# Attention scores taken out of the widened layer products, shifts in three rounds, in a three-layer graph attention kernel

## The chip, the cores and the metric

The kernel runs on one core of a Trainium2 chip. The metric is the time of the device in microseconds (us), the median of several runs; lower is better. The engines are TensorE (PE), VectorE (DVE), ScalarE (ACT), GpSimd (POOL) and SyncE (SP, which here only issues transfers). Each works through its own instructions in order, and they wait for one another by semaphores.

## The reference

1250 nodes with 768 features, 41250 edges and a self loop for each node. One dense layer gives x1; three graph attention layers (GAT) of four heads with 192 channels each all read x1, so there are 12 heads; their outputs are joined, multiplied by W_out, and added to x before a layer norm.

```python
def gat_conv(x, src, dst, W, a_src, a_dst, b):
    h = (x @ W).reshape(N, H, C)
    as_n = (h * a_src).sum(-1)
    ad_n = (h * a_dst).sum(-1)
    e = leaky_relu(as_n[src] + ad_n[dst], 0.2)
    m = segment_max(e, dst, num_segments=N)
    p = exp(e - m[dst])
    s = segment_sum(p, dst, num_segments=N)
    alpha = p / (s[dst] + 1e-16)
    out = segment_sum(alpha[:, :, None] * h[src], dst, num_segments=N)
    return out.reshape(N, H * C) + b
x1 = relu(x @ W_ah + b_ah)
xs = [relu(gat_conv(x1, src, dst, W, a_s, a_d, b)) for the three layers]
y = relu(concatenate(xs, axis=1) @ W_out + b_out)
return layernorm(x + y)
```

## The kernel before

The nodes are cut into 10 tiles of 125 (NT, PT), the 768 features into 6 blocks of 128 (KT, KP). The attention is dense: a matrix of edge counts (`cntT`, 1250 x 1250) and a mask (a very negative number where no edge is) are made once, then each head's weights are a full 1250 x 1250 matrix of exponentials times counts.

**Stage 1, to about 129 us.** PE counts edges into tiles and makes x1 (`x1_step`), in 18 groups: (m, 0) for all m, then (m, 1), (m, 2) in turn. ACT writes each group twice, as f32 (`x1T`) and rounded (`x1_hi`). DVE makes one-hot keys and then V = W a for each head (`reduce_v(l, k)`, eight reductions for each layer l and block k; SP loads the rows of W, three slots).

**Scores.** With V of all 12 heads (24 columns, source and destination), PE makes `scores(k)`: 36 f32 matmuls of x1T by V into `asadT`, 24 x 1250. ACT copies it out, SP stores the source rows to DRAM (`as_dram`), and PE turns it back to `asad` (nodes by heads) in `scores_turn`.

**Layer parts, 141.8 to 338 us.** `h_part(n)`, n = 0 to 5 (layer n // 2, half n % 2 of its columns): for each tile, 18 products of 384 columns into one PSUM bank (x_hi by W_hi, x_hi by W_lo, x_lo by W_hi, for 6 blocks). ACT copies each tile out, and after each odd tile issues two stores to `h_dram`. The weights of part n+1 are cast to `Wl_hi` by ACT (`round_w`, after tile ROUND_AT) from the raw ones, and DVE makes the rest (`rest_w`). The raw half of part n+2 is loaded after the last tile of part n. In part 0 stands an edge pass for windows with many edges (`more_counts`), a handshake of SP, DVE, PE and ACT.

**Maxima, on DVE beside the parts.** For each head a row of source scores is broadcast to all partitions (`asB`, SP's `load_as`), and 10 scans (L957) add the mask and take the maximum over the sources. Heads 0 to 9 (DEFER) come before the first shifts; heads 10 and 11 are scanned inside the first four pairs (`late_max`, five scans in each pair at LATE_AT).

**Shifts.** From the maxima DVE makes two numbers per node and head (`u`); PE turns them (`shifts`), ACT copies, SP stores to `u_dram` and broadcasts them back as rows (`load_u`). The first round, heads 0 to 9, is in part 5 after tile U_AT; the second, heads 10 and 11, before pair 4, where PE waits until ACT has copied the last features (`attT_sb`), because both use the same PSUM banks.

**Pairs of heads, 338 to 750 us.** For p = 0 to 5, 20 tiles each: DVE makes the exponent (`exponent_tile`), ACT the exponential, DVE the weight (`weight_tile`), PE 20 products of 193 columns (`tile`). There are two exponent slots and five weight slots. After each head DVE takes the sums (`invert`), ACT scales the head's output out of PSUM (`head_out`), and PE turns the features (`features`). Pairs 0 to 3 run in a loop on PE and ACT.

**End, 750 to 955 us.** W_out and the layer norm.

The order on each engine is written out by hand. The lines that the steps touch:

```python
def h_products(n, t, blocks):
    place = bank((2 * (n % 2) + t) % 4)[0:PT, 0:HALF]
    for k in blocks:
        if n == 0 and t == 0:
            pe.wait_ge(S["x1_lo"], k + 1)
            pe.wait_ge(S["w_lo"], 1)
        for i, (xx, ww) in enumerate(((x1_hi, Wl_hi), (x1_hi, Wl_lo), (x1_lo, Wl_hi))):
            ins = mm(place, xx[:, k, t * PT:(t + 1) * PT], ww[n][:, k], ...)
```

Of the kernel before, what the change touches and what calls it, by code (L numbers as in the profile page):

```python
# [14 lines left out]
PT = 125  # L15
# [27 lines left out]
V_HEAD = 1  # L43
G0_PARTS = 3
# [9 lines left out]
DEFER = LH - 2  # L54
TAKEN = 2 * NT // (PAIRS - 2)
# [3 lines left out]
ROUND_AT = 4  # L59
# [4 lines left out]
U_AT = 2  # L64
EXP_AT = NT - 3
# [36 lines left out]
def gnn_program(nc, x, xT_rows, dst, edges, W_ah, b_ah, W_all, a_all, b_all, W_out, b_out, out):  # L102
# [10 lines left out]
    with ExitStack() as ctx:  # L113
# [98 lines left out]
        asadT, _ = view(R_ROWS, 2 * N, 2 * LH, (N,))  # L212

        w_at = [(0, 7504)] + [(4808, 2504), (0, 7504)] * 2 + [(4808, 2504)]
        Wl_hi = [rounded("Wl_hi0", "R_EXP", 0, (KT, HALF))]
        Wl_hi += [rounded(f"Wl_hi{n}", "R_W", w_at[n][0], (KT, HALF)) for n in range(1, PARTS)]
        Wl_lo = [rounded(f"Wl_lo{n}", "R_W", w_at[n][1], (KT, HALF)) for n in range(PARTS)]
        w_raw = [view(R_W, w_at[n][1], KP, (KT, HALF))[0] for n in range(PARTS)]
# [63 lines left out]
        def out_at(q, t):  # L282
# [64 lines left out]
        def _(sp):  # L347
# [48 lines left out]

            def load_as(hh):
# [31 lines left out]
            for q in range(2):  # L429
                load_h(0, q)  # L430
            sp.wait_ge(S["h_ps"], NT * PARTS)
# [11 lines left out]
            with sp.Fori(1, PAIRS - 2) as p:  # L443
                load_pair(p)
            load_pair(PAIRS - 2)

            sp.wait_ge(S["uT_sb"], 2 * len(GROUPS))
            for w in range(2):
                rows = slice(w * LH + DEFER, (w + 1) * LH)
                sp.dma_start(u_dram[rows], uT2[rows]).then_inc(S["u_stored"], 16)  # L450
            sp.wait_ge(S["u_stored"], 16 * 3)
# [44 lines left out]
        def _(pool):  # L496
# [52 lines left out]
            pool.wait_ge(S["u_stored"], 16 * 3)  # L549
# [5 lines left out]
        def _(act):  # L555
# [84 lines left out]
            act.wait_ge(S["v_made"], 2 * HEADS * KT * LAYERS)  # L640
            act.wait_ge(S["asad_ps"], KT)
            for g, (t0, w) in enumerate(GROUPS):
                nc.scalar.copy(asadT[:, t0 * PT:(t0 + w) * PT], bank(2 + g)[0:2 * LH, 0:w * PT]).then_inc(S["asadT_sb"], 1)
            round_w(1)
# [25 lines left out]

            def h_part(n):

                l, c = n // 2, n % 2
                for t in range(NT):
                    i, slot = 5 * c + t // 2, (5 * c + t // 2) % 2
                    act.wait_ge(S["h_ps"], NT * n + t + 1)
                    if t % 2 == 0:

                        act.wait_ge(h_stored[slot], 32 * (NT // 2 * l + i // 2 + 1))
# [766 lines left out]
```

## Time and profile before

| | |
|---|---|
| Time before, median of 3 runs | 956.46 us (956.26 to 956.62) |
| Profiled execution | 956.7 us; span from its first to its last instruction 955.1 us |
| Granted TensorE clock, mean | 0.999 |
| PE busy | 933.2 us (98%) |
| DVE busy | 739.1 us (77%) |
| ACT busy | 367.5 us (38%) |
| DMA | 108.16 MB, mean 113 GB/s |

The profile is of one execution, the times are of others. Busy times are unions of overlapping instructions, and a matmul's record is longer than the step from one to the next, so counts and steps say more than means. "Idle before" is what the engine waited for, named by the one who released it. All times are us from the span's start unless marked ns.

### The profile page before, as it was taken

Reading aid. Unit: us, or ns where it says so; the run is one execution under the profiler, and the core shown is the slowest. Engines: PE = TensorE matmul, PEld = TensorE weight load, DVE = VectorE, ACT = ScalarE, POOL = GpSimd, SP = SyncE. Lnnn points to the kernel's source line nnn. Section 1 sums busy time; section 2 is a strip of 40 time slices with the busy share of each in tenths; the row PEclk is TensorE's granted clock in tenths of the full one; section 3 lists DMA queues with packets and bytes.
Section 4 is the critical chain, followed back from the end, with each engine's and each line's share of the span. In section 5 each row is a group of like instructions: output and inputs, shape, how many; then the busy total and the mean of one; then the engine's idle time right before and its main releaser. Section 6 shows DMA issues by size and latency. Waiting matters only on the chain.

```text
span 955.1 us, 14393 instructions
## 1 busy us (share of the span) xinstructions
PE 933.2 (98%) x5584; PEld 865.8 (91%) x5584; DVE 739.1 (77%) x1064; ACT 367.5 (38%) x534; POOL 45.9 (5%) x94
## 2 busy tenths in 40 slices
PE   6999999999999999999999999999999999999997
PEld 2677649999999999999999999999999779999996
DVE  6999986999999299998999999988877282243233
ACT  1666323122212255375465555555555540011000
POOL 4700000000000000000010010010010100000000
PEclk9999999999999999999999999999999999999999
DMA  5350722534453723144253352239341353223111
GB/s 174 50 197 22 259 85 89 168 108 152 130 163 92 227 75 95 56 108 106 82 123 63 94 131 67 71 101 374 93 121 42 101 161 127 81 91 116 68 33 33
DMA packets 57693, 108.16 MB, mean 113 GB/s; under 512 B 14013, under 2 KB 41246, under 8 KB 56487
## 3 DMA queue, kind: packets, MB, share of 16 engines
q1 hardware_dynamic: 39188, 66.22, 22.7%
q0 software_dynamic: 5360, 18.77, 7.7%
q10 hardware_dynamic: 13090, 22.44, 7.5%
q8 instruction: 34, 0.56, 0.2%
q14 instruction: 21, 0.16, 0.1%
HBM read 80.34 MB, written 27.08 MB: 112 GB/s over the span
## 4 chain that ended last, share of the span: by engine, by line
PE 56%; ACT 0%; DVE 0%; issue 0%; ACTq 0%
PE ps L1302 34%; PE ps L1382 18%; PE ps L1372 2%; PE ps L1337 2%; ACT R_XIN L733 0%; PE ps L1287 0%; DVE R_XIN L1118 0%; DVE stats L1108 0%; DVE R_EXP L1104 0%; DVE R_EXP L1102 0%; ACT rstd L785 0%; DVE mv L1113 0%; DVE rstd L1115 0%; ACTq L732 0%; ACTq L762 0%
## 5 line engine op out<-in xcount | busy, mean ns | idle before, releaser
L1302 PE MATMUL ps<-R_W 125*125 125x193 f32 x2400 | 395.2, 327 | 1.2 <-issue 0.8
L1302 PEld LDWEIGHTS ps<-R_W 125*125 125x125 f32 x2400 | 391.7, 188 | 1.8 <-issue 1.1
L707 ACT ACTIVATE R_W<-R_EXP,s 125x1250 f32<-125x1250 f32 x120 | 160.3, 1340 | 155.0 <-PE ps L1302 74.7
L998 DVE SCALAR_TENSOR_TENSOR R_W<-R_W,R_CNT 125x1250 f32<-125x1250 f32 x120 | 174.5, 1455 | 3.0 <-DVE R_EXP L987 1.7
L957 DVE CUSTOM_DVE_ANT_0 R_ROWS<-R_MASK,R_ROWS 125x1250 bf16<-125x1250 bf16 x100 | 138.6, 1456 | 3.2 <-ACTq L660 3.2
L1230 PE MATMUL ps<-Wl_hi,x_hi 128*125 128x384 f32 x360 | 122.1, 339 | 0.0
L1230 PE MATMUL ps<-Wl_hi,x_lo 128*125 128x384 f32 x360 | 121.7, 338 | 0.0
L1230 PE MATMUL ps<-Wl_lo,x_hi 128*125 128x384 f32 x360 | 121.6, 338 | 0.0
L1382 PE MATMUL ps<-Wo_hi,xs_hi 128*125 128x384 f32 (+2 forms) x324 | 109.5, 338 | 0.3 <-PE ps L1372 0.3
L1382 PE MATMUL ps<-Wo_lo,xs_hi 128*125 128x384 f32 (+2 forms) x324 | 109.4, 338 | 0.0
L1382 PE MATMUL ps<-Wo_hi,xs_lo 128*125 128x384 f32 (+2 forms) x324 | 109.2, 337 | 0.0
L987 DVE SCALAR_TENSOR_TENSOR R_EXP<-R_EXP,s 125x1250 f32<-125x1250 f32 x60 | 90.8, 1515 | 20.8 <-DMA R_EXP<-u_dram 12.3
L987 DVE SCALAR_TENSOR_TENSOR R_EXP<-R_X,s 125x1250 f32<-125x1250 f32 x60 | 90.7, 1511 | 13.4 <-ACT R_W L707 12.8
L1102 DVE TENSOR_TENSOR R_EXP<-ps,R_EXP 125x768 f32<-125x768 f32 (+2 forms) x11 | 9.7, 885 | 99.1 <-PE ps L1382 99.1
L680 ACT COPY R_HOUT<-ps 125x384 f32<-125x384 f32 x60 | 28.9, 481 | 140.3 <-PE ps L1230 138.7
L1174 PE MATMUL ps<-R_W 128*128 128x500 f32 (+1 forms) x180 | 74.8, 546 | 7.6 <-DMA R_W<-in_xT 7.6
L1230 PEld LDWEIGHTS ps<-Wl_hi,x_hi 128*125 128x125 f32 x360 | 66.8, 185 | 0.5 <-issue 0.4
L1230 PEld LDWEIGHTS ps<-Wl_lo,x_hi 128*125 128x125 f32 x360 | 66.7, 185 | 0.0
L1230 PEld LDWEIGHTS ps<-Wl_hi,x_lo 128*125 128x125 f32 x360 | 66.7, 185 | 0.0
L785 ACT ACTIVATE rstd<-mv,epsc 125x1 f32<-125x1 f32 x10 | 3.0, 296 | 158.6 <-DVE mv L1113 158.6
L1382 PEld LDWEIGHTS ps<-Wo_hi,xs_hi 128*125 128x125 f32 x324 | 60.0, 185 | 1.8 <-issue 0.9
L1382 PEld LDWEIGHTS ps<-Wo_lo,xs_hi 128*125 128x125 f32 x324 | 60.1, 185 | 0.9
(146 smaller groups left out, 824.8 us busy)
## 6 DMA issues: line engine op xcount, KB each, us to landing
xs_dram<-R_XIN POOLq DMA_DIRECT2D x18, 625.0 KB, 8.6
h_dram<-R_HOUT ACTq DMA_DIRECT2D x30, 336.0 KB
R_W<-h_dram SPq DMA_DIRECT2D x12, 840.0 KB
R_ROWS<-as_dram SPq DMA_DIRECT2D x12, 625.0 KB, 4.4
R_EXP<-u_dram SPq DMA_DIRECT2D x6, 1250.0 KB, 7.8
R_X<-u_dram SPq DMA_DIRECT2D x6, 1250.0 KB, 5.6
R_ROWS<-in_W_all SPq DMA_DIRECT2D x18, 384.0 KB, 3.4
Wo_sb<-in_W_out POOLq DMA_DIRECT2D x1, 6912.0 KB, 27.0
```

The costliest lines, as they stand in the source:

```text
L680: nc.scalar.copy(h_out[:, slot, t % 2 * HALF:(t % 2 + 1) * HALF], bank((2 * c + t) % 4)[0:PT, 0:HALF]).then_inc(S["h_sb"], 1)
L707: nc.scalar.activation(prob[r % PSLOTS], expo[:, r % XSLOTS], ACT.Exp, bias=s02[:, r % NT, ds(2 * p + r // NT, 1)]).then_inc(S["exp_done"], 1)
L957: nc.vector.tensor_tensor_reduce(out=masked[:, i % 2], in0=mask[:, b], in1=asB[0:PT, hh % 2], scale=1.0, scalar=NOBODY, op0=ALU.add, op1=A ...
L987: nc.vector.scalar_tensor_tensor(out=expo[:, r % XSLOTS], in0=uB[q][0:PT, 0], scalar=s08[:, r % NT, ds(2 * p + q, 1)], in1=uB[q][0:PT, 1], ...
L998: nc.vector.scalar_tensor_tensor(out=prob[r % PSLOTS], in0=prob[r % PSLOTS], scalar=HUGE, in1=cntT[:, r % NT, 0:N], op0=ALU.min, op1=ALU.m ...
L1102: nc.vector.tensor_tensor(yt_part, y_part, bo_part, ALU.add).then_inc(S["y_sum"], 1)
L1174: ins = mm(bank(5 + i % 3)[:, 0:w], W_ah_sb[m][:, k], xT[g][:, k], start=(k == 0), stop=(k == KT - 1))
L1230: ins = mm(place, xx[:, k, t * PT:(t + 1) * PT], ww[n][:, k], start=(k == 0 and i == 0), stop=(k == blocks[-1] and i == 2), skip_group_che ...
L1302: ins = mm(ps[0:PT, o:o + HW], prob[(q * NT + j) % PSLOTS][:, t * PT:(t + 1) * PT], hB[:, q, j], start=(j == 0 and t % 2 == 0), stop=(j == ...
L1337: ins = nc.tensor.transpose(bank(5 + i)[:, t * PT:(t + 1) * PT], att[:, g + t, k * KP:(k + 1) * KP], ident[0:PT, 0:PT])
L1372: ins = mm(ps[0:PT, o:o + HALF], xs_first[:, k] if k < early else xsT[:, k - early, 0:PT], Wo_sb[:, k, c * HALF:(c + 1) * HALF], start=(k ...
L1382: ins = mm(place, xx[i][:, k], ww[:, k, half], start=(k == 0 and n == 0), stop=(k == OK - 1 and n == 2))
```

## The change

- **Scores as columns.** `scores` and `scores_turn` go. V of the first two layers (heads 0 to 7, 16 columns) is set beside the weights of part 0, and V of layer 2 (heads 8 to 11, 8 columns) beside those of part 1, rounded and with a rest as the weights are (`round_v`, `rest_v`). The products of part 0 have 400 columns, those of part 1 392. ACT copies the score columns of each tile to `asad`; PE turns the source columns back (`source_turn`: eight tiles after tile 8 of part 0, two in the middle of the first tile of part 1, and ten after the first tile of part 2 for layer 2).
- **Order in part 0.** PE makes the x_hi terms of tiles 0 and 3 before it needs x1_lo; x1_lo is made for a group of tiles at a time (`rest_x1`), and V of layer 2 after V of the others, two of its blocks ahead of the edge pass and four behind it.
- **Weights.** The raw half of part n+1 is now loaded after tile 1 of part n, cast after tile 5 (ROUND_AT 5), and its rest is made at written-out places among the scans (REST_W_AT).
- **Shifts in three rounds.** Heads 0 to 7 after their 80 scans (turned in part 5 after tile 4), heads 8 and 9 in pair 1 (their 20 scans follow the first shifts), heads 10 and 11 before pair 4. Each of the later rounds has its turn on PE, copies on ACT, and two stores on SP.
- **First exponents.** `exponent_tile(0, 0)` and `(0, 1)` stand before the scans 6 and 7 of head 9, the weight tiles 0 and 1 before its scans 8 and 9.
- Pairs 0 and 1 are written out on PE and ACT, the loop runs over pairs 2 and 3.

```diff
-ROUND_AT = 4
+SCORED = [2 * ROUND_A, 2 * HEADS]
+REST_W_AT = {(0, NT - 1): 2, (3, 0): 3, (5, 0): 4, (7, 1): 5}
+EXP_IN = 6
+ROUND_AT = 5
+RAW_AT = 1
-U_AT = 2
-EXP_AT = NT - 3
+U_AT = 4
+EXP_AT = NT - 2
...
             def round_w(n):
-                act.wait_ge(S["w_in"], 16 * n + 16)
-                nc.scalar.copy(Wl_hi[n][:], w_raw[n]).then_inc(S["w_hi"], 1)
+                act.wait_ge(S["w_in"] if n else S["w_in_first"], 16 * max(n, 1))
+                nc.scalar.copy(Wl_hi[n][:, :, 0:HALF], w_raw[n]).then_inc(S["w_hi"], 1)
+            def round_v(n):
+                act.wait_ge(S["v_made"], 2 * HEADS * KT * (2 + n))
+                nc.scalar.copy(score_columns(n, Wl_hi), V_part[n]).then_inc(S["v_hi"], 1)
...
-                    if t == NT - 1 and n + 2 < PARTS:
-                        act.dma_start(w_raw[n + 2], w_half(n + 2)).then_inc(S["w_in"], 16)
-                    if t == ROUND_AT and 1 <= n < PARTS - 1:
+                    if t == RAW_AT and 1 <= n < PARTS - 1:
+                        act.dma_start(w_raw[n + 1], w_half(n + 1)).then_inc(S["w_in"], 16)
+                    if t == ROUND_AT and n < PARTS - 1:
                         round_w(n + 1)
...
+            dve.wait_ge(S["mask_ready"], 2 * NT + 1)
+            for hh in range(DEFER):
+                dve.wait_ge(asB_in[hh % 2], 16 * (hh // 2 + 1))
+                for b in range(NT):
+                    i = NT * hh + b
+                    if (hh, b) in REST_W_AT:
+                        rest_w(REST_W_AT[hh, b])
+                    if (hh, b) == (4, 0):
+                        slopes()
+                    if hh == DEFER - 1 and EXP_IN <= b < EXP_IN + XSLOTS:
+                        exponent_tile(0, b - EXP_IN)
+                    if hh == DEFER - 1 and b >= EXP_IN + XSLOTS:
+                        weight_tile(0, b - EXP_IN - XSLOTS)
...
+                if hh == ROUND_A - 1:
...
+                    shifts(0, ROUND_A, z)
...
+                    if late == (0, 1) and r == ROUND_B_AT:
+                        dve.wait_ge(S["uT_ps"], len(GROUPS))
+                        shifts(ROUND_A, DEFER, z)
...
             def h_part(n):
                 pe.wait_ge(S["w_hi"], n + 1)
-                if n > 0:
+                if n == 0:
+                    pe.wait_ge(S["v_hi"], 1)
+                    hi_terms(0)
+                    hi_terms(3)
+                    lo_terms(0).then_inc(S["h_ps"], 1)
+                    more_counts()
+                else:
                     pe.wait_ge(S["w_lo"], n + 1)
...
-            with pe.Fori(0, PAIRS - 2) as p:
+            pair(0, False)
+            pe.wait_ge(S["attT_sb"], 9 + 1)
+            shifts(2)
+            pair(1, False, nth=1)
+            with pe.Fori(2, PAIRS - 2) as p:
                 pair(p, False)
```

## Rows read from the trace of the kernel before

**Rows 1.** Stretches: us, then busy time of each engine (instructions), PE clock, DMA.
```profile
163.00:314.00 151.00, 151.00 (x861) 150.91 (x860) 146.66 (x205) 31.01 (x52) 0.14 (x1) 1.00 0.43 132
338.70:427.80 89.10, 88.64 (x551) 88.27 (x552) 87.91 (x76) 47.21 (x57) 1.96 (x2) 1.00 0.30 82
929.75:942.33 12.58, 12.58 (x56) 10.01 (x55) 3.99 (x7) 0.29 (x1) 0.00 (x0) 1.00 0.10 32
```

**Rows 2.** Chain that ended last, in order of time: start, us, what.
```profile
426.76 1.07 PE ps L1337 x10
...
632.46 0.44 PE ps L1337 x4
...
635.82 58.83 PE ps L1302 x360
```

**Rows 3.** Timeline of PE: start, us, line, out<-in, count, [idle before, releaser].
```profile
129.08 12.77 PE L1211 MATMUL ps<-R_X,u_place 128*24 128x500 f32 x36 [1.10 <-issue]
...
145.13 1.26 PE L1238 MATMUL ps<-ident,R_ROWS 24*125 24x24 f32 x10
...
148.01 1.12 PE L1131 MATMUL ps<-R_W 128*125 128x120 f16 x16
...
151.18 0.79 PE L1158 MATMUL ps<-ident,R_ROWS 125*125 125x125 f16 x10 [0.95 <-DVE R_ROWS L922]
...
408.67 3.54 PE L1302 MATMUL ps<-R_W 125*125 125x193 f32 x20 [0.46 <-ACT R_XIN L722]
```

**Rows 4.** Timeline of DVE.
```profile
128.90 2.56 DVE L928 TENSOR_TENSOR Wl_lo<-R_W,Wl_hi 128x2304 fp32r<-128x2304 f32 x1
...
144.16 0.18 DVE L853 CAST R_EXP<-R_EXP 128x32 f32<-128x32 int32 x1 [0.74 <-issue]
...
291.94 2.56 DVE L928 TENSOR_TENSOR Wl_lo<-R_W,Wl_hi 128x2304 fp32r<-128x2304 f32 x1 [1.51 <-ACT Wl_hi L633]
...
312.67 0.26 DVE L971 TENSOR_TENSOR u_place<-R_ROWS 125x100 f32<-125x100 f32 x1
...
325.19 2.95 DVE L987 SCALAR_TENSOR_TENSOR R_EXP<-R_EXP,s 125x1250 f32<-125x1250 f32 x2 [12.26 <-DMA R_EXP<-u_dram]
...
342.20 1.45 DVE L998 SCALAR_TENSOR_TENSOR R_W<-R_W,R_CNT 125x1250 f32<-125x1250 f32 x1
...
407.38 0.22 DVE L1008 TENSOR_SCALAR rsum<-ps 125x4 f32<-125x4 f32 x2
```

**Rows 5.** Timeline of ACT; ACTq is its queue of transfers.
```profile
128.39 0.46 ACT L605 ACTIVATE x_hi<-ps,b_ah_sb 128x250 fp32r<-128x250 f32 x1
...
178.62 0.48 ACT L680 COPY R_HOUT<-ps 125x384 f32<-125x384 f32 x1 [2.68 <-PE ps L1230]
179.13 0.81 ACTq L685 DMA_DIRECT2D h_dram<-R_HOUT  x2
...
289.78 2.12 ACT L633 CAST Wl_hi<-R_W 128x2304 fp32r<-128x2304 f32 x1
```

**Rows 6.** Groups by line, DVE: count, busy us, mean ns, idle before.
```profile
L957 DVE CUSTOM_DVE_ANT_0 R_ROWS<-R_MASK,R_ROWS 125x1250 bf16<-125x1250 bf16 x100 | 138.6, 1456 | 3.2 <-ACTq L660 3.2
...
L839 DVE CUSTOM_DVE_ANT_0 R_EXP<-R_ROWS 128x192 bf16<-128x192 f32 x96 | 27.1, 355 | 2.5 <-DMA R_ROWS<-in_W_all 2.5
```

**Rows 7.** Timeline of SP's queue of transfers.
```profile
130.90 0.34 SPq L393 DMA_DIRECT2D R_EXP<-in_edges  x1
...
143.26 0.36 SPq L403 DMA_DIRECT2D as_dram<-R_ROWS  x1
...
145.29 42.49 SPq L400 DMA_DIRECT2D R_ROWS<-as_dram  x4
```

**Rows 8.** DMA issues: count, KB each, median us to landing.
```profile
R_ROWS<-as_dram SPq DMA_DIRECT2D x12, 625.0 KB, 4.4
...
R_EXP<-in_edges SPq DMA_DIRECT2D x1, 16.0 KB, 2.8
```

**Rows 9.** Timeline of PE at the start.
```profile
7.63 3.67 PE L1174 MATMUL ps<-R_W 128*128 128x500 f32 x4 [7.63 <-DMA R_W<-in_xT]
```

More of the change, by code:

```diff
@@ L395, in _ @@
                                  ).then_inc(S["more_in"], 16)
+            for k in range(V_AHEAD, KT):
+                load_v(2, k)
             def load_as(hh):
@@ L430, in _ @@
                 load_h(0, q)
+            for hh in range(DEFER, LH):
+                load_as(hh)
             sp.wait_ge(S["h_ps"], NT * PARTS)
@@ L639, in _ @@
                     round_w(0)
[L640 to L644, printed above, removed]
+                    round_v(0)
             act.sem_inc(S["exp_done"], XSLOTS)
@@ new lines, in _, with slopes @@
+            reduce_v(2, V_TURN - 1)
+            more_counts()
+            rest_x1(1, 0, KT)
+            rest_x1(2, 0, KT)
+            for k in range(V_TURN, KT):
+                reduce_v(2, k)
+            rest_w(1)
+            rest_v(1)
+            def slopes():
+                dve.wait_ge(S["asad_sb"], 2 * NT)
+                nc.vector.tensor_scalar(s08[:], asad[:, :, 0:LH], 1.0 - SLOPE, None, ALU.mult)
+                link(nc.vector.tensor_scalar(s02[:], asad[:, :, 0:LH], SLOPE, None, ALU.mult))
+                dve.sem_inc(S["scores_ready"], 1)
@@ L972, in shifts @@
                 dve.sem_inc(S["amax_done"], 1)
-            for w in range(2):
-                link(nc.vector.memset(u[:, :, w * LH + DEFER:(w + 1) * LH], 0.0))
-            shifts(0, DEFER, z)
             def exponent_tile(p, r):
@@ L1217, in _, with h_product @@
             pe.wait_ge(S["mask_ready"], 2 * NT)
-            pe.wait_ge(S["v_made"], 2 * HEADS * KT * LAYERS)
-            for k in range(KT):
-                scores(k)
+            TERMS = ((x1_hi, Wl_hi), (x1_hi, Wl_lo), (x1_lo, Wl_hi))
+            def h_product(n, t, k, i, last):
+                xx, ww = TERMS[i]
+                return mm(bank((2 * (n % 2) + t) % 4)[0:PT, 0:w_wide[n]], xx[:, k, t * PT:(t + 1) * PT], ww[n][:, k],
+                          start=(k == 0 and i == 0), stop=last, skip_group_check=True)
@@ L1222, in h_products @@
             def h_products(n, t, blocks):
-                place = bank((2 * (n % 2) + t) % 4)[0:PT, 0:HALF]
                 for k in blocks:
-                    if n == 0 and t == 0:
-                        pe.wait_ge(S["x1_lo"], k + 1)
-                        pe.wait_ge(S["w_lo"], 1)
-                    for i, (xx, ww) in enumerate(((x1_hi, Wl_hi), (x1_hi, Wl_lo), (x1_lo, Wl_hi))):
-                        ins = mm(place, xx[:, k, t * PT:(t + 1) * PT], ww[n][:, k],
-                                 start=(k == 0 and i == 0), stop=(k == blocks[-1] and i == 2), skip_group_check=True)
@@ new lines, in h_products, with hi_terms, lo_terms @@
+                return ins
+            def hi_terms(t):
+                for i in range(2):
+                    if i == 1:
+                        pe.wait_ge(S["w_lo"], 1)
+                        pe.wait_ge(S["v_lo"], 1)
+                    for k in range(KT):
+                        h_product(0, t, k, i, False)
+            def lo_terms(t):
+                pe.wait_ge(S["x1_lo"], 1 + (t >= 4) + (t >= 8))
+                for k in range(KT):
+                    ins = h_product(0, t, k, 2, k == KT - 1)
+                return ins
@@ L1242, in more_counts, with source_turn @@
+            def source_turn(n, heads, groups):
+                for g, w in groups:
+                    pe.wait_ge(S["asad_sb"], NT * n + g + w)
+                    for tt in range(w):
+                        ins = nc.tensor.transpose(bank(5 + GROUPS.index((g, w)))[0:heads.stop - heads.start, tt * PT:(tt + 1) * PT],
+                                                  asad[:, g + tt, heads], ident[0:PT, 0:PT])
+                    ins.then_inc(S["asT_ps"], 1)
             def more_counts():
```

204 lines of the change are left out of this document (124 added, 80 removed).

## The prediction, before the result was known

> **What bounds the kernel now.** I read the stretches first [rows 1]. From 163 to 314 us, the body of the six layer parts, TensorE (PE) is busy in every us: 861 products in 151.0 us, 175.4 ns from one start to the next. From 338.7 to 427.8 (pair 0 of heads) it is busy for 88.64 of 89.10, but VectorE (DVE) is busy for 87.91: in this one pair both are full. The chain of waits confirms PE from pair 1 on [rows 2]. So us taken from PE count only if DVE, which makes the weights for the pairs, is earlier too. The PE timeline shows the one place where PE waits for it in pair 0: 0.46 us at 408.67 [rows 3], right after DVE's sums at 407.38 [rows 4]. DVE runs without a gap from the third weight tile (342.20, next start 343.57) to 407.38 [rows 4]. That chain is the second limit, and it sits almost on top of the first.
>
> **Step 1, PE up to part 4.** The 36 score matmuls start at 129.08 and last 12.77 us [rows 3]; V of all layers ends when 128.90 begins [rows 4], so V is just in time for them. Without them part 0 needs the last x1 copy (128.39 + 0.46 = 128.85 [rows 5]) and starts at about 128.95. Before, its first product stood at 141.78, where the score row ends: -12.8 us. The first weight half was cast by then, and V of layers 0 and 1 is there: layer 2's 48 reductions take 48 x 0.28 = 13.5 us [rows 6], so the others ended by 115.5. Group 0 of x1_lo is 3000 elements, 3.3 us at the rate of the 2304 in 2.56 [rows 4]; it, two blocks of layer 2's V and the first rest of the weights fit before 128.5. The last four blocks (9 us) come after the edge pass, by 157, and V's second cast at tile 7 of part 0, by 163; part 1 wants both at 168.
>
> The ten turns of the scores go: -1.3 [rows 3].
>
> Wider products: 54 products of 512 columns start within 12.58 us, 233.0 ns each (the row counts two neighbours at its edges too); against 175.4 for 384 that is 0.45 ns per column [rows 1]. 16 columns x 180 = +1.3 us, 8 x 180 = +0.6. From below, nothing (if the weight load set the pace); the 512s exclude it.
>
> The later edge pass is a handshake, and it loses its cover. Its edges are sent for at 130.90 [rows 7] and land 2.8 us later [rows 8], 133.7; SP does the same work up to there. DVE needs 3.85 us from its first key operation (144.16) to PE's edge product (148.01) [rows 3, 4]: 137.6. PE comes there after 39 products of 182.5 ns, at 136.2. So it waits 1.4 us where it waited for nothing. From there to the mask block is 3.17 us as before (151.18), whose 0.95 us wait stays, near 1.1. +1.5 in all; from 0.5 to 2.5 if the edges land 1 us off.
>
> Source turns: ten turns last 1.26 us, the first of them overlapped [rows 3]; eight, two and ten make 0.9 + 0.3 + 1.1 = +2.3. Each waits for a copy of a tile that was done before, so they stop nothing behind them.
>
> Sum at the start of part 4: -12.8 - 1.3 + 1.3 + 0.6 + 1.5 + 2.3 = **-8.4**.
>
> **Step 2, DVE up to the first shifts.** Scores leave with part 0's tiles, so all ten must be done: PE ends part 0 near 167.8, turns the last group in the middle of the next tile (169.6), ACT copies, SP stores and waits (2.03 us from its last store, 143.26, to the load at 145.29 [rows 7]), and the row lands 4.4 us after issue [rows 8]: the first maximum at about 176.6. Eight heads are 80 x 1.386 = 110.9 [rows 6], four rests of weights about 10, slopes and shifts 2.4: 299.5 if nothing waits.
>
> But rests wait for ACT's casts, which move from the fifth tile to the sixth (ROUND_AT 5), an odd one, with two stores first. The last one before: part 4's fifth-tile copy is followed by the cast from 289.78 to 291.90 [rows 5], and DVE waited 1.51 for it [rows 4]. After: one tile later (+3.16), the copy to the end of the stores +1.32 (178.62 to 179.94) instead of +0.37 [rows 5], and -8.4: 287.6. DVE itself would be there (the second scan of head 7) at 282.5 had it never waited; so it waits at the casts, 1 to 2 us each time, and the last cast sets it. A later first maximum, by up to 4 us, costs nothing. Then 2.5 + 9 scans 12.5 + shifts 1.9: shifts are done at **304.5**. Before: 312.67 + 0.26 = 312.93 [rows 4]. -8.4, as PE.
>
> **Step 3, from the shifts to pair 0.** Before, DVE then waited 12.26 us for the rows of u [rows 4]. Twenty scans (heads 8 and 9) are put there: +27.7, less what it waited. The third weight tile comes after 20 scans, five exponents and three weights. A pair of the two is 2.82 us (63.8 us from 343.57 to 407.38 less five scans and 0.45, by 20), so these are 3 x 2.82 + 2 x 1.45 = 11.3: 304.5 + 27.7 + 11.3 = 343.5, against 343.57. The gain is gone: the order brought 8.4 us, and the waits that twenty scans fill were that long and no longer. The rows of u are in time. Before, PE turned them after part 5's third tile, eight tiles of 3.16 us behind the copy that precedes the cast at 289.78: 314.7, and the exponent began at 325.19, 10.5 us later. Now it is the fifth tile, two more, less 8.4: 312.6 + 10.5 = 323.1; the first exponent is due at 326.7. SP has nothing in front of them but head 9's row, sent for at 302. On ACT the first exponential (x at 328.2) stands in front of the last tile's copy, which PE has ready only at 329.5.
>
> PE, free at about 330, gets weight tile 0 at 333.9 (18 scans, two exponents, one weight after 304.5), so it idles near 3.5 us, 0.5 before tile 1 and 2.5 before tile 2. Pair 0 keeps its five late maxima, so DVE runs on to the sums at 407.3, and PE, which would be back at 406.5, passes at 408.6. **-0.1.**
>
> **Step 4, the third round of shifts.** PE must wait until the last features are copied, then turn ten tiles. Before, it does this once: the last features start at 632.46, pair 4 goes on at 635.82; without a round they last 1.07 (426.76) [rows 2]. 635.82 - 632.46 - 1.07 = **+2.3**. It is bare PE time in the pair boundary, and DVE does not bind there. DVE's own shifts (1.9) in pair 1 stand before tiles that PE wants only after its pause; ACT's and SP's parts lie in slack (SP's store of u stands before a load that waits for DVE anyway), and POOL, whose load of W_out now waits for five stores, is past them by then. If PE's features were copied earlier the price would be 1.2, if the pause met another wait it would be 3.5.
>
> **Sum.** -0.1 + 2.3 = +2.2 us. The profiled execution was 956.7 us (span 955.1), so 958.9; the median of the runs was 956.46: **958.5 us**. 0.2% is 1.9 us, about what can be told from no change.
>
> **A rule against the change.** The first four x1 matmuls, after 7.63 us of idle, took 3.67 us, 0.92 each [rows 9], and 500 columns settle at 0.42 later (12.77 us for 24 of 500 and 12 of 250 in [rows 3]): half the speed, the 1.2 GHz level instead of 2.4 (the granted clock of the whole run is 0.999, so it says little of so short a stretch). The new waits of 3.5 and 2.5 us could bring this back in pair 0. Lost then: 2.0 us, as there, to 3.5. PE has 2.1 us to spare up to 408.6, so 0 to 1.4 us would show.
> The Trainium skill, "TensorE: Matmul & The Clock Gate", section "Part 1: The HAM clock gate", says that an idle array goes back to the half clock and earns the full one by steady work; by it the time would be up to 959.9. Whether the trace agrees can't be read from it: after the start PE waits 1.1 us at most.
>
> **Rivals.**
> 1. *The casts don't hold DVE.* If they come before DVE does, the shifts are ready at 299.5 to 302.5 and everything in step 3 is 2 to 5 us earlier. PE then passes at 403.6 to 406.6: -2.1 + 2.3 = +0.2, down to -5.1 + 2.3 = -2.8. 953.6 to 956.7. For it: waits of 1 to 2 us are near my error. Against: before, two casts already held DVE by 1.4 and 1.5 us, at a tile earlier.
> 2. *PE keeps its gain* (the other side): DVE doesn't bind in pair 0, because its late maxima or weights find room. Then -8.4 + 2.3 = -6.1: 950.4. The 0.46 us at 408.67 speaks against it; it decides as soon as the sums come more than 1.9 us earlier than 407.3.
> 3. *A hand-over is late*: the first row of sources after 181, u after 326.7, or the clock above. Each us late passes through DVE to pair 0. +1.5 to +4 on the sum: 960 to 962.5.
> 4. *The edge pass waits longer than 1.4 us*: part of my range, +1.
>
> **How the numbers follow.** The chain as worked out, 956.8 to 959.8, has 0.48: the error is a us on the casts and half a us on the pause. Rival 3 with 4: 0.22. Rival 1: 0.18. Rival 2: 0.12. Range **953.6 to 962.5**: out are rival 2, a little of rival 1 and the end of rival 3, under 2 in 10. Below 954.5 lie rival 2 and a part of rival 1: faster 0.20. Above 958.4 lie half of the likeliest case and rival 3: slower 0.44. The rest, 0.36, is within 0.2%. Likeliest by itself: 956.8 to 959.8.
>
> **What would show it.** Part 0's first product near 129; a PE wait of 1.4 us before the edge product and 1 before the mask block; PE ahead by 8.4 us at part 4; the last cast ending near 287.6 and a DVE wait before each rest of weights; shifts done at 304.5; PE idle for some 3.5 us near 330; the sums of pair 0's second head at 407.3; pair 1's pause of 1.1 us and ten turns. I am wrong if shifts come before 302, if PE isn't idle before its first head tile, or if the pause is hidden.

## The result, and the profile after

The changed kernel takes 957.99 us (median of 22 runs, 957.61 to 959.05) against 956.20 (median of 22, 955.28 to 956.62): ratio 1.0021, 95% interval 1.0016 to 1.0027. So it is slower by 1.8 us, right at the 0.2% that the prediction took as the bound. Predicted were 958.5, in the likeliest case 956.8 to 959.8, in all 953.6 to 962.5. Of all the executions in this text one, of the kernel with narrow late maxima, took 2448 us; it is left out of its median.

The profiled execution has a span of 956.3 us (before 955.1). In it the last copy of x1 begins at 127.66, in before's at 128.39 [rows 5]. In the twelve other executions profiled below it begins anywhere from 127.28 to 129.05, so these 0.73 us are taken to belong to the execution and not to the change, and are put back where two times are compared ("so counted"). The change does move some loads and small operations ahead of that moment; no run tests them alone.

The timeline of TensorE (PE) in the changed kernel, where the edge pass, the start of pair 0 and the pass to pair 1 lie. "The pass" is the short wait at 407.62, where the banks of the last head must be free; the first 24 products of pair 1 stand just ahead of it. Products are counted by their records in the profile: the f32 matmuls of the pairs leave two each, so the 20 products of a weight tile are ten matmuls of the kernel (2400 records for 1200 of them).

```profile
128.34 1.32 PE L1302 MATMUL ps<-Wl_hi,x_hi 128*125 128x400 f32 x6 [1.08 <-issue]
136.83 1.17 PE L1217 MATMUL ps<-R_W 128*125 128x120 f16 x16 [1.09 <-DVE R_W L923]
140.06 0.79 PE L1244 MATMUL ps<-ident,R_EXP 125*125 125x125 f16 x10 [0.91 <-DVE R_EXP L980]
...
327.99 0.34 PE L1302 MATMUL ps<-Wl_hi,x_lo 128*125 128x384 f32 x1
332.85 8.29 PE L1418 MATMUL ps<-R_W 125*125 125x193 f32 x40 [4.52 <-DVE R_W L1058]
342.67 30.33 PE L1418 MATMUL ps<-R_W 125*125 125x193 f32 x184 [1.53 <-DVE R_W L1058]
373.48 32.95 PE L1418 MATMUL ps<-R_W 125*125 125x193 f32 x200 [0.48 <-ACT R_XIN L777]
407.62 9.42 PE L1418 MATMUL ps<-R_W 125*125 125x193 f32 x56 [1.19 <-ACT R_XIN L777]
...
427.83 1.24 PE L1403 MATMUL ps<-ident,u_place 125*24 125x125 f32 x10 [1.06 <-ACT R_XIN L788]
```

The layer parts are done at 328.33. Then stand a gap of 4.52 us, two weight tiles, a gap of 1.53 before the third, and two short ones (0.48 and 1.19) where ScalarE (ACT) copies a head out after VectorE's (DVE's) sums. The same stretch in the kernel before, read now from its timeline of PE:

```profile
337.58 0.34 PE L1230 MATMUL ps<-Wl_hi,x_lo 128*125 128x384 f32 x1
338.68 69.52 PE L1302 MATMUL ps<-R_W 125*125 125x193 f32 x424 [0.77 <-issue]
408.67 9.42 PE L1302 MATMUL ps<-R_W 125*125 125x193 f32 x56 [0.46 <-ACT R_XIN L722]
```

There all 424 products up to the pass run in one piece, 164.0 ns each. From the last product of the layer parts to the pass into pair 1 before needs 408.67 - 337.92 = 70.75 us, after 407.62 - 328.33 = 79.29. That is where the gain of the layer parts went: 8.54 us. Of it 3.75 are the first gap (4.52 - 0.77), 1.53 the second, 1.21 those at the sums (0.48 + 1.19 - 0.46), and 1.73 are the first 40 products, which took 8.29 in place of 6.56; 0.3 is left. A piece ends with a record that is longer than a step (28 products at the full clock took 4.84 us in the run with the gap filled, 0.25 more than 28 x 164.0 ns), so of the 1.73 nearer 1.5 are the clock's. The windows of the changed kernel show why the 40 were slow; the column after the busy times of the five engines is PE's granted clock:

```profile
332.00:333.00 1.00, 0.15 (x1) 0.18 (x2) 1.00 (x2) 0.00 (x0) 0.00 (x0) 0.76 0.96 299
333.00:334.00 1.00, 1.00 (x4) 1.00 (x5) 1.00 (x1) 0.00 (x0) 0.00 (x0) 0.50 0.93 357
334.00:335.00 1.00, 1.00 (x5) 1.00 (x4) 1.00 (x3) 0.00 (x0) 0.00 (x0) 0.50 0.38 138
335.00:336.00 1.00, 1.00 (x5) 1.00 (x4) 1.00 (x2) 0.00 (x0) 0.00 (x0) 0.54 0.00 0
336.00:337.00 1.00, 1.00 (x8) 1.00 (x7) 1.00 (x3) 0.00 (x0) 0.00 (x0) 1.00 0.00 0
```

By finer windows the granted clock is 0.50, the 1.2 GHz level, from about 332.5 to 335.9, that is from within the gap; the expectations below put it at 332.8 to 335.5.

The timeline of DVE in the changed kernel, against [rows 4]:

```profile
175.21 1.46 DVE L1089 CUSTOM_DVE_ANT_0 R_ROWS<-R_MASK,R_ROWS 125x1250 bf16<-125x1250 bf16 x1 [13.53 <-DMA R_ROWS<-as_dram]
190.33 2.56 DVE L993 TENSOR_TENSOR Wl_lo<-R_W,Wl_hi 128x2304 fp32r<-128x2304 f32 x1 [2.61 <-ACT Wl_hi L668]
223.29 2.56 DVE L993 TENSOR_TENSOR Wl_lo<-R_W,Wl_hi 128x2304 fp32r<-128x2304 f32 x1 [1.41 <-ACT Wl_hi L668]
254.88 2.56 DVE L993 TENSOR_TENSOR Wl_lo<-R_W,Wl_hi 128x2304 fp32r<-128x2304 f32 x1 [0.85 <-ACT Wl_hi L668]
...
303.06 0.24 DVE L1036 TENSOR_TENSOR u_place<-R_ROWS 125x80 f32<-125x80 f32 x1
...
341.16 1.46 DVE L1058 SCALAR_TENSOR_TENSOR R_W<-R_W,R_CNT 125x1250 f32<-125x1250 f32 x1
342.53 1.51 DVE L1047 SCALAR_TENSOR_TENSOR R_EXP<-R_EXP,s 125x1250 f32<-125x1250 f32 x1
...
406.32 0.22 DVE L1068 TENSOR_SCALAR rsum<-ps 125x4 f32<-125x4 f32 x2
```

DVE waits at three rests of weights for ACT's casts (the fourth cast ends at 286.49, just as DVE comes to it), then works through: the third weight tile's successor starts at 342.53 (before 343.57), the sums at 406.32 (before 407.38). The 12.26 us for which DVE stood before u [rows 4] are filled to the last.

And the chain of waits of the changed kernel, at the boundary of pairs 0 and 1, where before had a plain 426.76 [rows 2]:

```profile
425.71 0.44 PE ps L1453 x4
...
426.17 0.68 ACT R_XIN L788 x2
426.85 0.45 issue
427.31 0.48 ACT R_XIN L788
...
427.83 1.24 PE ps L1403 x10
429.07 58.83 PE ps L1418 x360
```

429.07 - 425.71 - 1.07 = 2.29 us for the third round.

### The profile page after: what moved, and what is told of

The parts are those of the page before. It is cut to its first block, busy times and chain, and to the rows that moved or that the text cites. A ratio compares the mean times of both kernels' runs of the same rounds, so it can differ in the third digit from the quotient of the medians.

```text
span 956.3 us, 14226 instructions
## 1 busy us (share of the span) xinstructions
PE 924.9 (97%) x5568; PEld 865.9 (91%) x5568; DVE 739.5 (77%) x1068; ACT 371.9 (39%) x562; POOL 45.8 (5%) x94
## 4 chain that ended last, share of the span: by engine, by line
PE 56%; ACT 0%; DVE 0%; issue 0%; ACTq 0%
PE ps L1418 34%; PE ps L1502 18%; PE ps L1492 2%; PE ps L1453 2%; ACT R_XIN L788 0%; PE ps L1403 0%; DVE R_XIN L1204 0%; DVE stats L1194 0%; DVE R_EXP L1188 0%; DVE R_EXP L1190 0%; ACT rstd L843 0%; DVE mv L1199 0%; DVE rstd L1201 0%; ACTq L787 0%; ACTq L820 0%
## 5 line engine op out<-in xcount | busy, mean ns | idle before, releaser
L1302 PE MATMUL ps<-Wl_hi,x_hi 128*125 128x384 f32 (+2 forms) x360 | 116.4, 341 | 1.1 <-issue 1.1
L1302 PE MATMUL ps<-Wl_lo,x_hi 128*125 128x384 f32 (+2 forms) x360 | 115.8, 340 | 0.0
L1302 PE MATMUL ps<-Wl_hi,x_lo 128*125 128x384 f32 (+2 forms) x360 | 115.7, 340 | 0.0
```

The lines of the kernel that those rows point to most:

```text
L1302: return mm(bank((2 * (n % 2) + t) % 4)[0:PT, 0:w_wide[n]], xx[:, k, t * PT:(t + 1) * PT], ww[n][:, k], start=(k == 0 and i == 0), stop=la ...
```

## The experiments

Each edit is made on the changed kernel, except one. Times are medians; "to before" is the difference to the kernel before, run beside it, "to changed" that less 1.79. The intervals of the ratios are 0.8 to 1.3 us wide to either side, so differences of less than that between two runs are read from the traces, not from the medians.

| run | us | ratio to before (95%) | to before | to changed |
|---|---|---|---|---|
| casts earlier | 955.42 | 0.9990 (0.9981 to 0.9999) | -0.65 | -2.4 |
| no third round | 955.89 | 1.0000 (0.9991 to 1.0009) | -0.18 | -2.0 |
| narrow scans | 954.25 | 0.9980 (0.9971 to 0.9989) | -1.82 | -3.6 |
| edges first | 956.67 | 1.0006 (0.9997 to 1.0015) | +0.60 | -1.2 |
| turns later | 955.45 | 0.9994 (0.9985 to 1.0002) | -0.67 | -2.5 |
| gap filled | 958.38 | 1.0020 (1.0012 to 1.0029) | +2.26 | +0.5 |
| narrow late maxima | 955.98 | 0.9998 (0.9989 to 1.0007) | -0.14 | -1.9 |
| narrow scans, u and exponents earlier | 949.51 | 0.9928 (0.9915 to 0.9941) | -6.61 | -8.4 |
| narrow scans, u earlier | 954.14 | 0.9978 (0.9969 to 0.9987) | -1.85 | -3.6 |
| three edits together | 951.44 | 0.9949 (0.9935 to 0.9962) | -4.55 | -6.3 |
| the three, u earlier, third tile first | 951.35 | 0.9949 (0.9936 to 0.9963) | -4.64 | -6.4 |
| before, with its turn later | 954.73 | 0.9988 (0.9979 to 0.9997) | -1.26 | |

### Casts one tile earlier

```diff
-ROUND_AT = 5
+ROUND_AT = 4
```

> Only the place of the casts of a weight half is changed: behind the even tile 4 of a layer part in place of tile 5, one tile or about 3.2 us earlier. Theory A (the casts hold VectorE, and VectorE's third weight tile sets pair 0): in the changed kernel the rests waited 2.61, 1.41 and 0.85 us for casts that stand on TensorE's time; with each cast 3.1 to 3.2 us earlier the chain of scans, exponents and weights comes 2.8 to 3.2 us earlier at the third weight tile (339.5 in place of 342.5), TensorE's gap of 4.5 us shrinks to about 1.5, and the time falls from 958.0 to 954.8 to 955.4. Theory B (the casts are no gate; what binds is TensorE's own work or the scans' sum): no change, 957.7 to 958.3. Theory C (the granted clock of 0.5 behind the 4.5 us gap is what costs): the gap shrinks and the time falls by the same 3 us but by another 1.4 beside it, to 953.5.

-2.4 us, 955.42, at the upper edge of theory A. Two of the three waits went; the timelines of DVE and PE in this run:

```profile
251.50 2.56 DVE L993 TENSOR_TENSOR Wl_lo<-R_W,Wl_hi 128x2304 fp32r<-128x2304 f32 x1 [0.85 <-ACT Wl_hi L668]
...
322.72 1.52 DVE L1047 SCALAR_TENSOR_TENSOR R_EXP<-R_EXP,s 125x1250 f32<-125x1250 f32 x1 [0.35 <-DMA R_EXP<-u_dram]
...
331.94 1.46 DVE L1058 SCALAR_TENSOR_TENSOR R_W<-R_W,R_CNT 125x1250 f32<-125x1250 f32 x1 [0.75 <-ACT R_W L762]
```

```profile
340.56 64.69 PE L1418 MATMUL ps<-R_W 125*125 125x193 f32 x384 [2.27 <-DVE R_W L1058]
405.51 9.42 PE L1418 MATMUL ps<-R_W 125*125 125x193 f32 x56 [0.26 <-ACT R_XIN L777]
```

The rest that waited 0.85 us at 254.88 now waits the same 0.85 at 251.50: it is the cast that sets DVE there. So the casts hold DVE, and DVE holds pair 0. In this execution the last x1 copy began 0.81 us later than in the changed kernel's, so the cast (249.28 against 252.66) is 4.2 us earlier by its own chain: the tile and, on ACT, two stores that no longer stand ahead of it. The third tile is 2.11 + 0.81 = 2.9 earlier, since 0.35 go to waiting for u and 0.75 to ACT, the next gates. From the third tile to the pass PE needs 405.51 - 340.56 = 64.95 us, as in the changed kernel (407.62 - 342.67 = 64.95), to a hundredth.

That is more telling than it looks, since the two stretches differ inside. The granted clock, at 1.00 up to 340.5 in this run, falls behind the gap of 2.27 us and stays low to 343.9:

```profile
340.00:341.00 1.00, 0.44 (x1) 0.44 (x2) 1.00 (x2) 0.51 (x1) 0.00 (x0) 0.79 1.01 415
342.00:343.00 1.00, 1.00 (x5) 1.00 (x5) 1.00 (x1) 1.00 (x1) 0.00 (x0) 0.50 0.05 20
```

So the 384 products take 64.69 us, 1.7 more than 384 x 164.0 ns, where the changed kernel has its gaps of 0.48 and 1.19. DVE sets the pass, and PE's loss lies in its slack. The low clock is thus moved in this run, not removed, and what speaks against theory C is this equal stretch, not its absence.

### Without the third round

```diff
-            pe.wait_ge(S["attT_sb"], 9 + 1)
-            shifts(2)
-            pair(1, False, nth=1)
+            pair(1, False)
...
-            store_u(1, ROUND_A, DEFER)
...
-                    if late == (0, 1) and r == ROUND_B_AT:
-                        dve.wait_ge(S["uT_ps"], len(GROUPS))
-                        shifts(ROUND_A, DEFER, z)
```

(the counts of the last round follow.)

> The shifts of heads 8 and 9 are left out (TensorE's ten turns, the copies, the stores and VectorE's six small operations between pairs 0 and 1), so those two heads get shifts of zero. Theory A (a round costs TensorE a pause of 1.06 and ten turns of 1.24 with nothing beside it): minus 2.3 us, 955.5 to 955.9, just under the kernel before. Theory B (the pause and the turns lie beside work of VectorE, which would hold TensorE in pair 1 anyway): minus 0.5 us or less. In the trace under A the product behind the last feature turn of pair 0 starts within 0.2 us of it.

-2.0 us, with 2.3 expected and none under theory B. In its trace the pause and the turns between pairs 0 and 1 are gone. The round's 2.29 us are bare.

### Narrow scans

```diff
-                    nc.vector.tensor_tensor_reduce(out=masked[:, i % 2], in0=mask[:, b], in1=asB[0:PT, hh % 2], scale=1.0,
-                                                   scalar=NOBODY, op0=ALU.add, op1=ALU.max,
+                    m, least = (N, NOBODY) if hh < ROUND_A else (PT, 0.0)
+                    nc.vector.tensor_tensor_reduce(out=masked[:, i % 2, 0:m], in0=mask[:, b, 0:m], in1=asB[0:PT, hh % 2, 0:m], scale=1.0,
+                                                   scalar=least, op0=ALU.add, op1=ALU.max,
```

> The last twenty full scans (heads 8 and 9) look at 125 of 1250 columns with a floor of zero, so each costs about 0.25 in place of 1.37 us and those heads' shifts are other values. It takes some 22 us of VectorE's work away between 300 and 335 us. Theory A (TensorE's gain of some 9 us in the layer parts is lost to VectorE, which is late by the gap before pair 0 and then paces pair 0): TensorE passes from the layer parts into pair 0 with no gap over 0.5 us, 424 products at 0.164 us end near 399 in place of 406.4, and the time falls by 7 to 8 us to 950 to 951. Theory B (the gap is a wait for the shifts' way through memory, landed at 322.9, and for ScalarE): the gap stays over 2 us and the time falls by under 4. Theory C (pair 0 is bound by its weight tiles whatever came ahead): minus 1.5 at most.

A miss: with 22 us of DVE's work away only 3.6 of the expected 7 to 8 us came, and PE kept gaps of 0.77, 1.40 and 1.10. The scans are one gate; a second stands right behind them. Timelines of DVE and of ACT in this run:

```profile
322.37 1.52 DVE L1047 SCALAR_TENSOR_TENSOR R_EXP<-R_EXP,s 125x1250 f32<-125x1250 f32 x1 [14.94 <-DMA R_EXP<-u_dram]
...
327.32 1.46 DVE L1058 SCALAR_TENSOR_TENSOR R_W<-R_W,R_CNT 125x1250 f32<-125x1250 f32 x1 [1.58 <-ACT R_W L762]
...
331.54 1.46 DVE L1058 SCALAR_TENSOR_TENSOR R_W<-R_W,R_CNT 125x1250 f32<-125x1250 f32 x1 [2.55 <-ACT R_W L762]
```

```profile
325.94 1.35 ACT L762 ACTIVATE R_W<-R_EXP,s 125x1250 f32<-125x1250 f32 x1
328.73 0.48 ACT L726 COPY R_HOUT<-ps 125x384 f32<-125x384 f32 x1 [1.44 <-PE ps L1303]
329.24 0.81 ACTq L731 DMA_DIRECT2D h_dram<-R_HOUT  x2
330.17 1.34 ACT L762 ACTIVATE R_W<-R_EXP,s 125x1250 f32<-125x1250 f32 x1 [0.96 <-ACT R_HOUT L726]
```

Two suspects: u comes through memory at 322.37, and the second exponential, whose input DVE had ready by 325.5, stands on ACT behind the last tile's copy and its stores, at 330.17. Two more runs tell them apart, both with the narrow scans:

```diff
-U_AT = 4
+U_AT = 2
-EXP_AT = NT - 2
+EXP_AT = NT - 4
```

> As the run with narrow scans, and TensorE's turn of the first shifts stands behind tile 2 in place of tile 4 of the last layer part, and ScalarE's first two exponents behind its tiles 6 and 7 in place of 8 and 9. With narrow scans alone VectorE stood 14.94 us waiting for the shifts' way through memory, which starts with that turn, and TensorE still had gaps of 0.77, 1.40 and 1.10 us. Theory A (behind the scans stands a second gate at almost the same time, the turn that TensorE makes at a place fixed in its own order, and the exponents' place on ScalarE): the gaps fall to under 0.5 us together, and the time is 3 to 4 us under the run with narrow scans alone, 950.3 to 951.3. Theory B (what is left is pair 0 itself, with or without a gap ahead): no more than 0.5 under that run.

> As the run with narrow scans, and of the two edits that gave 4.7 us more only the first: the first shifts turned behind tile 2 in place of 4 of the last part; ScalarE's first two exponents stay behind its tiles 8 and 9. Theory A (with VectorE's scans gone the gate is the exponents' place on ScalarE: the first stood directly behind the copy of tile 8 at 325.57 and the second behind that of tile 9 and its stores, at 330.17, and weight tile 1 at 331.54 waited for it): no change against narrow scans alone, 953.9 to 954.6. Theory B (the gate is the shifts' way through memory, 14.94 us of waiting on VectorE): most of the 4.7 us comes back, 949.5 to 950.5.

With both edits PE never waits in pair 0 for a weight tile; its timeline is that of the kernel before, 9.4 us earlier:

```profile
329.23 69.52 PE L1419 MATMUL ps<-R_W 125*125 125x193 f32 x424 [0.77 <-issue]
399.23 9.42 PE L1419 MATMUL ps<-R_W 125*125 125x193 f32 x56 [0.47 <-ACT R_XIN L777]
```

949.51 us, 8.4 under the changed kernel and lower than expected: the whole gain of the layer parts. With the turn of u alone (`U_AT`) the time is 954.14, as with narrow scans alone, and DVE's wait only changes its name, in its timeline:

```profile
317.84 1.52 DVE L1047 SCALAR_TENSOR_TENSOR R_EXP<-R_EXP,s 125x1250 f32<-125x1250 f32 x1 [9.70 <-DMA R_EXP<-u_dram]
327.86 1.46 DVE L1058 SCALAR_TENSOR_TENSOR R_W<-R_W,R_CNT 125x1250 f32<-125x1250 f32 x1 [6.64 <-ACT R_W L762]
```

So behind the scans it is the exponentials' place in ACT's order that binds first, not the way through memory. Whether the exponentials' place alone, without the earlier u, would give all of it was not tried.

### Edges first

```diff
-            sp.dma_start(w_raw[1], w_half(1)).then_inc(S["w_in"], 16)
             more, each = passes(sp)
...
+            sp.dma_start(w_raw[1], w_half(1)).then_inc(S["w_in"], 16)
```

> SyncE issues the load of the edge pass ahead of the second weight half in place of behind it. In the changed kernel VectorE waited 5.59 us for those edges and TensorE 1.09 us before the edge product. Theory A (a chain in lockstep: TensorE's start of the parts sets the casts, the casts set VectorE, VectorE sets pair 0): the edges land 2 to 3 us earlier, the wait of 1.09 goes, everything to the third weight tile comes 1.0 to 1.2 us earlier, and the time is 956.8 to 957.1. Theory B (VectorE has its own pace to pair 0, and what TensorE gains in the parts is only a longer gap at 328): the gap grows from 4.5 to 5.6 and the time stays at 958.0 within 0.3.

-1.2 us, theory A. PE's wait before the edge product is gone from its list of waits, and the third tile starts 1.02 us earlier (1.3 with the 0.28 by which x1 was later in this execution), with the same gaps ahead of it:

```profile
331.83 8.32 PE L1419 MATMUL ps<-R_W 125*125 125x193 f32 x40 [4.52 <-DVE R_W L1059]
341.65 30.33 PE L1419 MATMUL ps<-R_W 125*125 125x193 f32 x184 [1.50 <-DVE R_W L1059]
```

The gap did not grow. About a us taken from PE ahead of part 1 is handed on by the casts to DVE, and by DVE to pair 0. That is why the prediction's steps 1 and 2 have the same sum, -8.4.

### Turns later

```diff
+                    if nth is not None and r == FEAT + 1:
+                        pe.wait_ge(S["attT_sb"], 9 * p + 1)
+                        shifts(nth + 1)
                     tile(p, r)
...
-            pe.wait_ge(S["attT_sb"], 9 + 1)
-            shifts(2)
...
-            pe.wait_ge(S["attT_sb"], 9 * (PAIRS - 2) + 1)
-            shifts(3)
```

> TensorE's turns of the second and third round stand one weight tile later, behind the first products of the next pair and not right behind the last feature turn. All the work stays. Theory A (each round costs a pause of 1.06 us, in which TensorE waits for ScalarE's features, and 1.24 for ten turns): the two pauses go and the turns stay, minus 2.0 to 2.2 us, 955.8 to 956.1. Theory B (the pause only moves, since the product behind it would wait for a weight tile or a bank as well): 957.7 to 958.2.

-2.5 us. Both pauses of 1.06 are gone from its timeline and the turns stay; they account for 2.1, and the 0.4 beyond lie within what the medians can tell. The same edit on the kernel before, which has one such round:

> The kernel before, with TensorE's turn of its second and last round one weight tile later, behind the first products of the next pair. Theory A (the pause of 1.06 us at the round is no property of the change, each round of either kernel has it): minus 1.0 to 1.3 us, 954.8 to 955.1. Theory B (the pause comes back as a wait for a weight tile or a bank): 955.9 to 956.3.

-1.26 us. The turns stand there, in its timeline of PE, between products with no idle ahead:

```profile
631.97 3.43 PE L1302 MATMUL ps<-R_W 125*125 125x193 f32 x20
635.24 1.23 PE L1287 MATMUL ps<-ident,u_place 125*24 125x125 f32 x10
```

### The gap filled

```diff
             pe.wait_ge(S["uT_sb"], len(GROUPS))
+            for _ in range(38):
+                nc.tensor.transpose(bank(5)[0:PT, 0:PT], ident[0:PT, 0:PT], ident[0:PT, 0:PT])
```

> TensorE does 38 turns of the identity, which nothing uses, in the gap of 4.5 us between the layer parts and the first weight tile of pair 0. Theory A (the granted clock of 0.50 from about 332.8 to 335.5 us is lent out of slack, since TensorE waits for the third weight tile anyway): the clock stays at 1.00, the second gap grows from 1.5 to about 2.9 us, and the time stays at 958.0 within 0.4. Theory B (the low clock is in the time): the time falls by 1.2 to 1.5 us.

The windows and the timeline of this run:

```profile
333.00:334.00 1.00, 0.62 (x4) 0.65 (x5) 1.00 (x2) 0.00 (x0) 0.00 (x0) 1.00 0.93 361
...
345.00:346.00 1.00, 1.00 (x5) 1.00 (x4) 1.00 (x2) 0.94 (x1) 0.00 (x0) 0.50 0.00 0
```

```profile
343.20 64.70 PE L1420 MATMUL ps<-R_W 125*125 125x193 f32 x384 [2.27 <-DVE R_W L1058]
408.14 9.42 PE L1420 MATMUL ps<-R_W 125*125 125x193 f32 x56 [0.25 <-ACT R_XIN L777]
```

The clock stays at 1.00 over the first two tiles, they are done earlier, the gap before the third is 2.27 (0.51 more stand before the second), and the pass comes 64.94 us after the third tile as ever. The median is 0.5 above the changed kernel, within 0.9.

But the turns only put the low clock off: it comes at 344.4, 1.2 us into the third tile, and lasts to 347.7. So this run alone does not show what a kernel without it would take. It shows that the low clock ahead of the third tile costs nothing: that tile starts at 343.20, which is 342.60 with the 0.60 taken off by which the last x1 copy was later than in the changed kernel's execution, against 342.67 there. And behind the third tile the stretch to the pass is 64.94 with the low clock in it and 64.95 without (changed kernel, and narrow scans). The low clock is in the trace but not in the time, in either place.

### Narrow late maxima in pair 0

```diff
-                nc.vector.tensor_tensor_reduce(out=masked2[:, j], in0=mask[:, b], in1=asB[0:PT, pp], scale=1.0,
-                                               scalar=NOBODY, op0=ALU.add, op1=ALU.max,
+                m, least = (PT, 0.0) if (pp, e) == (0, 0) else (N, NOBODY)
+                nc.vector.tensor_tensor_reduce(out=masked2[:, j, 0:m], in0=mask[:, b, 0:m], in1=asB[0:PT, pp, 0:m], scale=1.0,
+                                               scalar=least, op0=ALU.add, op1=ALU.max,
```

> The five late maxima in pair 0 look at 125 of 1250 columns with a floor of zero, about 0.25 in place of 1.37 us each, so that head 10 has other shifts. It takes 5.6 us out of VectorE's 63.8 between the third weight tile and the sums of pair 0. Theory A (pair 0 is bound by both engines: after the third weight tile TensorE has only 0.48 and 1.19 us of gaps, at the sums of its two heads): minus 1.0 to 1.7 us. Theory B (VectorE alone paces pair 0): minus 4 to 5.6 us. Theory C (it is TensorE): no change.

-1.9 us, a little past theory A's range: of 5.6 us of DVE's work a third shows. In its timeline PE goes through from the third tile on:

```profile
342.45 72.17 PE L1419 MATMUL ps<-R_W 125*125 125x193 f32 x440 [0.43 <-DVE R_W L1058]
```

440 products in one piece, 164.0 ns each; the 384 from the third tile to the pass would need 63.0 us where DVE's pace makes them 64.95. Both engines are full in pair 0, DVE by 2 us more.

### Together

The three edits that leave all the work in place (casts earlier, edges first, turns later):

> The three edits together: casts one tile earlier, edges ahead of the second weight half, the turns of both later rounds behind the next weight tile. All the work stays. Theory A (three terms of one chain, each in another place: VectorE's start of pair 0, TensorE's start of the parts that moves the casts too, TensorE's two pauses): the measured gains add up, 2.6 + 1.3 + 2.5 = 6.4 under the changed kernel, 951.3 to 952.0, and 4 to 5 under the kernel before. Theory B (with the casts earlier VectorE already stood 0.35 us waiting for the first shifts, so that gate takes part of the edges' gain): 952.5 to 953.

951.44 us, theory A: 4.6 us under the kernel before and 6.3 under the changed one. The sum of the three alone is 6.1. Then two more edits:

```diff
-U_AT = 4
+U_AT = 3
...
-            for r in range(EARLY + 1):
-                exponent_tile(0, r + XSLOTS)
-                if r >= NT - EXP_IN - XSLOTS:
-                    weight_tile(0, r)
+            exponent_tile(0, 2)
+            exponent_tile(0, 3)
+            weight_tile(0, 2)
+            exponent_tile(0, 4)
```

> As the run with the three edits, and two more: the first shifts are turned behind tile 3 in place of 4 of the last layer part, and VectorE does the third weight tile of pair 0 ahead of the fifth exponent, not behind it. Theory A (in every run whose pair 0 starts late, TensorE took 64.95 us from its third tile to the pass to pair 1 with 62.8 of products in them, so VectorE's sum of work sets the end of pair 0 and an earlier third tile alone gives nothing; only the 0.35 us of waiting for the shifts come back): 0.2 to 0.5 us under the run with the three edits. Theory B (the third weight tile's own time sets pair 0): the swap gives 1.4 us more, 1.6 to 1.9 us under it.

951.35, no gain that can be measured. The earlier third tile gives nothing, as theory A said. Its 0.35 us did not come either. DVE's timeline, weight tile 1, in the run with three edits and in this one:

```profile
330.49 1.46 DVE L1059 SCALAR_TENSOR_TENSOR R_W<-R_W,R_CNT 125x1250 f32<-125x1250 f32 x1 [0.75 <-ACT R_W L763]
```

```profile
330.55 1.46 DVE L1059 SCALAR_TENSOR_TENSOR R_W<-R_W,R_CNT 125x1250 f32<-125x1250 f32 x1 [1.19 <-ACT R_W L763]
```

The wait for u (0.35) went and the wait for the second exponential grew by 0.44: again ACT's order.

## Why the prediction was right

**Step 1, PE (-8.4).** 8.9 by the trace: the last products of the layer parts start at 337.58 and 327.99, less 0.73. The 0.45 more are the edge pass: its waits are 1.09 and 0.91 where 1.4 and 1.1 were forecast and 0 and 0.95 stood before.

**Step 2, DVE (shifts done at 304.5).** Measured 303.06 + 0.24 = 303.30, and 304.03 with the 0.73. The first maximum was put at 176.6, measured 175.94 so counted. The waits at the casts, "1 to 2 us each time", are 2.61, 1.41 and 0.85, shrinking from cast to cast; at the last one, which was to end near 287.6 and ends at 287.22 so counted, DVE arrives together with it and hardly waits. That the casts set DVE is shown by the run with earlier casts.

**Step 3 (-0.1).** The weight tile that was due at 343.5 ends at 343.26 so counted, the pass at 408.35 where 408.6 was forecast. -0.3 in place of -0.1. PE's gaps were forecast as 3.5, 0.5 and 2.5 and came as 4.5, none and 1.5. The first is longer mainly because PE is free at 329.06 so counted, a us before the "about 330" of the step. The other two are shorter because the half clock stretched the two tiles between them: in the run with the gap filled, where it did not, they are 0.51 and 2.27. The step named DVE's work as what takes the gain. That is half of it: with the scans narrow 3.6 us come back, with ACT's exponentials moved too 8.4. The step had looked at ACT only to see that the first exponential is not in the way, and missed that the second one stands behind the last copy. The number didn't suffer: in the changed kernel DVE comes later than this gate, which begins to show (0.75 us) when DVE is some 3 us earlier, in the run with earlier casts. The expectation of the narrow scans did.

**Step 4 (+2.3).** 2.29 in the trace, -2.0 when it is left out.

**Sum (+2.2).** -0.3 + 2.3 = 2.0, measured 1.8.

**The rule against the change.** The trace agrees with the Trainium skill's "TensorE: Matmul & The Clock Gate", section "Part 1: The HAM clock gate": in a gap of 4.5 us without work the granted clock falls to 0.50, the 1.2 GHz level, until 335.9. It takes 1.5 to 1.7 us from two tiles, where 2.0 to 3.5 were set for it. But the term in the time was 0 of the forecast 0 to 1.4: PE waits for its third tile anyway.

**Rivals.** 1 (the casts don't hold DVE): refuted by the earlier casts, -2.4. 2 (PE keeps its gain, 950.4): that is the time that was reached, 949.5, once both gates were taken away; in the changed kernel neither was. 3 (a late hand-over): none came; u was there, and the clock is hidden. 4 (a longer wait at the edge pass): it is shorter, but the run with the edges first shows that its us would have counted.

## What to carry to other kernels

An engine's us count only as far as the next hand-over lets them: before taking work from the busiest engine, find the stretch in which the second one is full as well, and see which instructions of all engines stand in front of its first tile. A gap that is filled with new work is spent, and behind one gate another may stand (here DVE's scans, then ACT's order, 3.6 of 8.4 us on); taking one away shows only the distance to the next. A turn that waits for another engine's last copy loses its pause if one tile of independent work is put in front of it: 1.2 to 1.3 us for each round here, in either kernel. And an effect that is gone where it was may have moved: the low clock stood a few us later in the runs with earlier casts and with the gap filled.

## What the runs showed of the hardware

The granted clock near the start of pair 0, read in windows of a us or less in every profiled execution (before and with both gates gone it never fell):

| runs | PE's gaps, us | granted clock of 0.50 |
|---|---|---|
| changed kernel | 4.52 | 332.5 to 335.9, from within the gap |
| narrow late maxima, same work ahead | 4.52 | 331.1 to 338.0, from within the gap |
| casts earlier | 0.81, 1.35, 2.27 | 340.6 to 343.9, as the third tile starts |
| gap filled | 0.39, 0.51, 2.27 | 344.4 to 347.7, from 1.2 us into the third tile |
| narrow scans | 0.77, 1.40, 1.10 | never |

The other runs with a gap of 4.5 us (no third round, edges first, turns later) lost the clock in the gap or with the first product behind it; the three edits together, with 0.82, 1.34 and 2.27, lost it 1.0 us into the third tile. So in three runs the clock fell although the longest gap near it was 2.27 us, and it fell when PE was at work again.

With the same gap the price to PE varies: the 40 products behind it took 8.29, 8.32 and 8.45 us in three runs, 9.02 and 9.39 in two (no third round, narrow late maxima), where the low clock lasted twice as long. None of it is in the time here. With gaps of 1.53, 0.80, 1.36, 2.27 and 0.43 us just before it, the third tile starts between 342.56 and 342.79, with each run's last x1 copy set to the changed kernel's 127.66 (changed kernel, no third round, turns later, gap filled, narrow late maxima). The last of these had only 0.43 us to spare.
